# One unit order, one peeled group and one DMA queue changed in an attention and FFN kernel

## The reference

```python
x = x + xattn(layernorm(x), ctx, ctx, pos, mask, Wq, Wk, Wv, Wo)   # x, ctx: 8 x 256 x 1024
x = x + ffn(layernorm(x), qweight, qzeros, scales, bias)           # 1024 -> 1024
# xattn
q = (x @ Wq) -> 32 heads of 128;  k, v = (ctx @ Wk), (ctx @ Wv) -> 8 heads of 128
q, k = q * cos[pos] + rotate_half(q) * sin[pos], the same for k
scores = where(mask == 0, -1e9, q @ k.T / sqrt(128))   # each k, v head serves 4 query heads
return (softmax(scores) @ v) @ Wo
# ffn
return x @ (scales * (4-bit weights - zeros)) + bias
```

## Time and profile before

| what | value |
|---|---|
| median of 3 executions | 2343.98 us (2342.11 to 2347.69) |
| the profiled execution's own time | 2343.98 us |
| PE busy | 2248.4 us, 96% |
| DVE, ACT, POOL busy | 1351.8 us (58%), 1042.3 us (45%), 1379.2 us (59%) |
| DMA moved | 493.52 MB, mean 211 GB/s |

### The profile page before, as it was taken

The page is one execution under the profiler, slowest core; times in us unless marked ns, Lnnn a source line. Parts: engine busy times, 40 slices in busy tenths (PEclk is TensorE's granted clock), DMA queues, the critical chain, the costliest instruction groups (busy, mean ns, idle before and its releaser), DMA issues.

```text
span 2342.2 us, 33158 instructions
## 1 busy us (share of the span) xinstructions
PE 2248.4 (96%) x10560; PEld 1870.0 (80%) x10560; DVE 1351.8 (58%) x2534; ACT 1042.3 (45%) x2264; POOL 1379.2 (59%) x981
## 2 busy tenths in 40 slices
PE   8998999988999999799999999889999999999999
PEld 6887877767888887688888888668887877878887
DVE  4762574767777776577777777537723234443532
ACT  3222123666766675566677667523322222322000
POOL 1320454567888887688888888655654354354220
PEclk9999999999999999999999999999999999999999
DMA  7676675788788778877878887687554454452111
GB/s 270 234 192 208 229 265 184 235 271 275 241 246 252 242 244 278 281 243 242 255 236 250 250 246 246 189 257 267 189 196 158 148 188 153 152 179 99 46 45 45
DMA packets 310494, 493.52 MB, mean 211 GB/s; under 512 B 28176, under 2 KB 200464, under 8 KB 310416
## 3 DMA queue, kind: packets, MB, share of 16 engines
q1 hardware_dynamic: 289680, 440.12, 58.8%
q10 hardware_dynamic: 19968, 50.34, 6.2%
q0 software_dynamic: 768, 2.10, 0.3%
HBM read 312.09 MB, written 180.37 MB: 210 GB/s over the span
## 4 chain that ended last, share of the span: by engine, by line
PE 65%; DMA 9%; POOL 8%; DVE 8%; issue 3%; ACT 3%; SPq 3%; ACTq 0%; POOLq 0%; DVEq 0%
PE ps L227 14%; PE ps L228 14%; PE ps L229 14%; PE ps L763 8%; PE ps L765 8%; PE ps L764 8%; DMA sq_scratch<-scores 5%; POOL q_t L1540 2%; DMA scores<-in_ctx 2%; POOL rope_tmp L1482 2%; SPq L426 1%; DVE rows L1386 1%; POOL s_buf L1482 1%; POOL q_t L1529 1%; DMA left_scratch<-s_buf 1%
## 5 line engine op out<-in xcount | busy, mean ns | idle before, releaser
L227 PE MATMUL ps<-act_t,wq_t 128*128 128x512 f32 x1280 | 502.4, 393 | 8.5 <-DVE wq_t L1302 4.1
L228 PE MATMUL ps<-act_t,wq_t 128*128 128x512 f32 x1280 | 501.2, 392 | 0.0
L229 PE MATMUL ps<-act_t,wq_t 128*128 128x512 f32 x1280 | 499.2, 390 | 0.0
L763 PE MATMUL ps<-b_parts,a_parts 128*128 128x512 f32 x896 | 353.3, 394 | 17.1 <-POOL b_parts L1558 11.0
L1540 POOL TENSOR_TENSOR q_t<-pt_raw,q_t 128x1024 fp32r<-128x1024 f32 x124 | 298.1, 2404 | 112.1 <-ACT q_t L962 111.1
L1558 POOL TENSOR_TENSOR b_parts<-wraw,b_parts 128x512 fp32r<-128x512 f32 x112 | 195.0, 1741 | 276.2 <-ACT b_parts L984 276.2
L1280 DVE TENSOR_TENSOR a_parts<-xring,a_parts 128x1024 fp32r<-128x1024 f32 x112 | 147.4, 1316 | 355.2 <-ACT a_parts L979 355.2
L764 PE MATMUL ps<-b_parts,a_parts 128*128 128x512 f32 x896 | 350.1, 391 | 0.0
L765 PE MATMUL ps<-b_parts,a_parts 128*128 128x512 f32 x896 | 350.0, 391 | 0.0
L979 ACT ACTIVATE a_parts<-xring 128x1024 fp32r<-128x1024 f32 x112 | 118.7, 1060 | 421.7 <-PE ps L765 413.2
L227 PEld LDWEIGHTS ps<-act_t,wq_t 128*128 128x128 f32 x1280 | 242.2, 189 | 57.7 <-issue 4.7
(11 more groups left out here) (120 smaller groups left out, 4344.4 us busy)
## 6 DMA issues: line engine op xcount, KB each, us to landing
sq_scratch<-scores SPq DMA_DIRECT2D x124, 512.0 KB, 4.9
pt_raw<-sq_scratch SPq DMA_DIRECT2D x496, 128.0 KB, 3.1
xring<-left_scratch SPq DMA_DIRECT2D x112, 512.0 KB, 4.0
left_scratch<-s_buf SPq DMA_DIRECT2D x64, 640.0 KB, 5.1
wraw<-in_L_xattn_Wq SPq DMA_DIRECT2D x64, 512.0 KB, 4.8
wraw<-in_L_xattn_Wo SPq DMA_DIRECT2D x64, 512.0 KB, 4.8
v_scratch<-kv_t ACTq DMA_DIRECT2D x32, 512.0 KB, 2.9
k_scratch<-kv_t ACTq DMA_DIRECT2D x32, 512.0 KB, 4.8
```

The source lines that it names most:

```text
L227: eng.matmul(dst, lh, rh, start=(k == first), stop=False)
L228: eng.matmul(dst, lh, rl, start=False, stop=False)
L229: mm = eng.matmul(dst, ll, rh, start=False, stop=(k == last))
L763: pe.matmul(dst, lh, rh, start=(begins and not onto), stop=False, skip_group_check=True)
```

## The change

It has four parts.

1. The pieces: all eight now pass in group 0, one in each unit. SP loads piece u8 at the end of unit u8, ACT stores the parts of piece u8-1 in unit u8 and splits piece u8 at its end. Group 1 is no longer peeled and joins the loop.
2. On ACT, `turned_hi` of the unit before now stands ahead of `query_hi` and `exponents`, in every unit of every group, instead of behind `exponents`.
3. On DVE, `next_head_lo` now stands behind `out_copy` and `inverse_sum`, instead of ahead of them.
4. The 16 loads of the new activations in group 7 are issued by SP, at the start of `u8` 2 and 4, instead of by ACT in the middle of these units.

```diff
@@ -444,12 +444,21 @@
                     sp.wait_ge(parts_stored, i * 32)
                 sp.dma_start(x_pair[0], xc_dram[i]).then_inc(xc_in, 16)
 
-            def attention(G, half, first=False, last=False, switch=False, piece=None):
+            def attention(G, half, first=False, last=False, switch=False):
                 g, nh = (0, 1) if switch else (G - half * 8 + 1, half)
                 for u8 in range(UPG):
                     par, b = u8 // 4, u8 % 4
                     p = (G - half * 8) * 2 + par
                     tail = last and par == 1
+                    if switch and u8 in (2, 4):
+
+                        c = u8 // 2 - 1
+                        sp.wait_ge(q_done, 62 + 2 * c)
+                        sp.wait_ge(parts_stored, 8 * 32)
+                        for k in range(4):
+                            for l in range(2):
+                                sp.dma_start(act_v[:, l, 2 * k:2 * k + 2, c * CT:(c + 1) * CT].bitcast(F32),
+                                             xp_dram[4 * c + k, l]).then_inc(xp_in[4 * c + k], 16)
 
                     if last and u8 == 1:
                         load_step(0)
@@ -486,8 +495,8 @@
                             c = (u8 - 3) // 2
                             sp.wait_ge(q_rot, 62 + 2 * c)
                             sp.dma_start(rope[:, c, :, :], rope_dram[1, c]).then_inc(rope_in[c], 16)
-                    if piece is not None and u8 % 2 == 1 and piece + u8 // 2 < 7:
-                        load_centred(piece + u8 // 2 + 1)
+                    if first and u8 > 0:
+                        load_centred(u8)
                 if last:
                     load_step(2)
                     load_step(3)
@@ -527,9 +536,8 @@
 
             sp.wait_ge(x_lo, TT)
             load_centred(0)
-            attention(0, 0, first=True, piece=0)
-            attention(1, 0, piece=4)
-            with sp.Fori(2, 7) as G:
+            attention(0, 0, first=True)
+            with sp.Fori(1, 7) as G:
                 attention(G, 0)
             attention(7, 0, switch=True)
             with sp.Fori(8, 15) as G:
@@ -983,7 +991,7 @@
                     act.wait_ge(right_in[s % 2], rights_in(s))
                 act.activation(b_parts[:, s % 2, 0, :], wraw[s % 2][:, 0:NW], ACT.Copy).then_inc(right_hi, 1)
 
-            def attention(G, first=False, last=False, switch=False, piece=None):
+            def attention(G, first=False, switch=False, last=False):
                 for u8 in range(UPG):
                     b = u8 % 4
                     tail = last and u8 >= 4
@@ -992,22 +1000,18 @@
                         head_hi(1, G * 32 + (u8 // 4 * 16 + 10 * 16), (q_done, G * UPG + (u8 + 4)))
                     if b == 3 and not last:
                         head_hi(0, G * 32 + (u8 // 4 * 16 + 11 * 16), (q_done, G * UPG + (u8 + 4)))
-                    if piece is not None and u8 % 2 == 1:
-                        store_parts(piece + u8 // 2)
+                    if last and u8 <= 4 or not last:
+                        if u8 > 0:
+                            turned_hi(G, u8 - 1, first=first and u8 < 3)
+                        elif not first:
+                            turned_hi(G - 1, UPG - 1)
+                    if first and u8 > 0:
+                        store_parts(u8 - 1)
                     if not (last and u8 >= 5):
                         i = (u8 + 3) % 4
 
                         scored = G * 16 + (2 * (u8 + 1 - i) + (0 if i < 2 else 4))
                         query_hi(TILES[i], G * UPG + (u8 + 3), None if first and u8 == 0 else scored)
-                    if switch and u8 in (2, 4):
-
-                        c = u8 // 2 - 1
-                        act.wait_ge(q_done, 62 + 2 * c)
-                        act.wait_ge(parts_stored, 8 * 32)
-                        for k in range(4):
-                            for l in range(2):
-                                act.dma_start(act_v[:, l, 2 * k:2 * k + 2, c * CT:(c + 1) * CT].bitcast(F32),
-                                              xp_dram[4 * c + k, l]).then_inc(xp_in[4 * c + k], 16)
                     if u8 < UPG - 1:
                         nxt, nG = u8 + 1, G
                     else:
@@ -1019,19 +1023,14 @@
                         elif not (first and u8 == 0):
                             act.wait_ge(squared, G * UPG + u8)
                         exponents(nG, nxt)
-                    if last and u8 <= 4 or not last:
-                        if u8 > 0:
-                            turned_hi(G, u8 - 1, first=first and u8 < 3)
-                        elif not first:
-                            turned_hi(G - 1, UPG - 1)
                     if tail:
                         tail_high(u8)
                     if last and u8 in (5, 6):
                         step_hi(u8 - 5)
                     if not (last and u8 == UPG - 1):
                         scaled(nG, nxt)
-                    if piece is not None and u8 % 2 == 0:
-                        split_piece(piece + u8 // 2)
+                    if first:
+                        split_piece(u8)
 
 
             act.wait_ge(ident_in, 16)
@@ -1043,9 +1042,9 @@
             exponents(0, 0)
             scaled(0, 0)
             act.wait_ge(rope_stored, 32)
-            attention(0, first=True, piece=0)
-            attention(1, piece=4)
-            with act.Fori(2, 7) as G:
+            attention(0, first=True)
+            store_parts(UPG - 1)
+            with act.Fori(1, 7) as G:
                 attention(G)
             attention(7, switch=True)
             with act.Fori(8, 15) as G:
@@ -1310,7 +1309,7 @@
                     op = dve.tensor_tensor(lo, ps[:, bank, :].rearrange("p (a n) -> p a n", a=4), hi.bitcast(F32), ALU.subtract)
                 op.then_inc(tail_lo, 1)
 
-            def attention(G, half, first=False, switch=False, last=False, piece=None):
+            def attention(G, half, first=False, switch=False, last=False):
                 for u8 in range(UPG):
                     b = u8 % 4
                     tail = last and u8 >= 4
@@ -1326,10 +1325,6 @@
                         nxt, nG, nh = 0, G + 1, 1 if switch else half
                     if not (last and u8 == UPG - 1):
                         masked(nG, nxt, nh, fresh=first and u8 == 0 or last and nxt >= 6)
-                    if b == 0 and not tail:
-                        next_head_lo(1, G * 4 + (2 * (u8 // 4) + 20))
-                    if b == 3 and not last:
-                        next_head_lo(0, G * 4 + (2 * (u8 // 4) + 21))
                     if tail:
                         if u8 < 6:
                             out_copy(G, u8 - 2)
@@ -1346,8 +1341,12 @@
                         set_mask(u8 - 3, 1)
                     if tail:
                         tail_low(u8)
-                    if piece is not None and u8 % 2 == 0:
-                        rest_of_piece(piece + u8 // 2)
+                    if b == 0 and not tail:
+                        next_head_lo(1, G * 4 + (2 * (u8 // 4) + 20))
+                    if b == 3 and not last:
+                        next_head_lo(0, G * 4 + (2 * (u8 // 4) + 21))
+                    if first:
+                        rest_of_piece(u8)
                     if last and u8 in (6, 7):
                         step_lo(u8 - 6)
 
@@ -1361,9 +1360,8 @@
                 query_rot(m % 2, FIRST_TILES[m][1], m, first=(m == 0))
             masked(0, 0, 0, fresh=True)
             inverse_sum(0, 0)
-            attention(0, 0, first=True, piece=0)
-            attention(1, 0, piece=4)
-            with dve.Fori(2, 7) as G:
+            attention(0, 0, first=True)
+            with dve.Fori(1, 7) as G:
                 attention(G, 0)
             attention(7, 0, switch=True)
             with dve.Fori(8, 15) as G:
```

## The result

The changed kernel takes 2444.2 us (median of 4 runs, 2441.5 to 2444.6); the kernel before took 2343.1 us beside it (median of 4, 2337.7 to 2347.7). The ratio is 1.043, 95% interval 1.041 to 1.045: slower, by about 101 us. The forecast was 2395 us with a range up to 2436, so the direction was right and the size was half of what came.

A forecast was written before the change was run, and what follows sets the result against it. The prediction took PE's own pace, 8.26 us a unit, as the bound over most of the kernel. It summed 2344 + 29 (pieces) + 26 (loops) - 4 (switch) = 2395 us, with an 8-in-10 range of 2358 to 2436.

The forecast's parts named there:

- a chain of 16.0 us a link: Group 0: each piece's split, rest, store and next load follow in series, 16.0 us a link, seven links.
- The term was +29: Pieces in group 0: PE starts unit 24 at 659.1 instead of 630.21, +29 us, with +16 and +47 as ends.
- 13 x 2.0 = +26 us: Loops: `turned_hi` ahead of `query_hi` makes the query and one unit 2.0 us late in each of 13 groups.
- SP's lead: Loops: SP's chain falls behind PE over six units and catches up at `u8` 3, having no head, key or value to load.
- The upper end: Loops, parts 2 and 3 together: a two-unit loop with slow landings in every unit, 71.4 us a group, +69 us.
- rival 2: Loops: the two-unit loop binds in every group, +69 instead of +26, total 2438 us; chance 0.12.
- a loop of two units through DRAM: Loops: `turned_hi`, exponentials, scaling, transposes through DRAM, next `turned_hi`: 17.0 us for two units, 18.7 with the head's split, against 16.5.
- -4 forecast: Switch, loads on SP: -1.0 us for each of two batches, about -2 from SP's earlier second lot, -4 us in all.
- 931.7: Switch: time near which the squares' store lands behind SP's eight loads, against 929.15 before, 2.6 us later.
- 941: Switch: time at which SP comes to the second batch of loads, where ACT came at 943.05; about -2 us.
- Rival 3: Switch gets worse, both issue times on SP's chain and both stores late: +18 instead of -4, total 2417 us; chance 0.07.
- The likeliest case: The forecast itself, 2395 us, with +26 for the loops; own range 2375 to 2420, chance 0.52.

The follow-up runs named there:

- Part 1 alone: All eight pieces in group 0, one in each unit, group 1 joining the loop, on the kernel before: 2375.8 us, ratio 1.014.
- part 2 alone: On ACT, `turned_hi` moved ahead of `query_hi` and the exponentials in every unit, on the kernel before: 2407.8 us, ratio 1.026.
- parts 2 and 3: `turned_hi` ahead of `query_hi` and DVE's head split behind the inverse, on the kernel before, pieces and switch unchanged: 2418.1 us, ratio 1.031.
- part 3 alone: DVE's head split (`next_head_lo`) moved behind `out_copy` and `inverse_sum`, on the kernel before: 2342.3 us, ratio 0.998.
- part 4 taken back: The changed kernel with the 16 loads of the switch issued by ACT again instead of SP: 2444.7 us, ratio 1.041.

## Why the prediction fell short

**The pieces: right, but the close hit is in part luck.** Forecast a chain of 16.0 us a link, measured 15.2; PE at unit 24 forecast 659.1, measured 660.9. In between two errors cancel: unit 9, forecast at 535.2, came at 526.6, 8.6 us early, and the 15 units from there to unit 24, forecast at 123.9 us, took 134.3. The term was +29. Part 1 alone gives +28. In the changed kernel groups 0 to 2 take 261.0 us for 227.1, +33.9; less twice 4.6 for the loop's loss in groups 1 and 2 (their units have no pieces, so it should stand there too; that is an inference) it is +24.7.

**The loops: this is the step that failed.** "I count 13 groups (1 to 6 and 8 to 14): 13 x 2.0 = +26 us." The mechanism named, ACT's wait for `pt_raw` holding the query and PE waiting for L1529, is what the run of part 2 alone shows. Its count was wrong, and a second way to PE was left at nothing. Part 2 alone measured +60, parts 2 and 3 +70, a group of the loop 3.7 and, in the changed kernel, 4.6 us instead of 2.0. Two things were missed:
- I took the delay of one unit, `u8` 3, from one row, and supposed that SP's lead heals it once a group. In the run of part 2 alone the lateness is in four units a group, 0.6 to 1.1 us each. A wait that costs nothing in the old order says how late the data comes, not how often; for that all the `turned_hi` of a group were to be read.
- For the sum I followed only the first instruction behind the wait, the query. The exponents stand behind it too, and DVE waits for them at the inverse. Behind the inverse stands the next rotation: `turned_hi` behind the query alone costs +42, and moving the inverse away takes back 40 of it. In the changed kernel the head's split stands there as well, and in its two late units (`u8` 1 and 5) PE waits for it 1.5 us on average.

**The upper end and rival 2 came near by luck.** The upper end had +69 for the two edits, and +70 was measured; rival 2 said 2438, and 2444 came. Its reason was a loop of two units through DRAM. For the 42 us that reason is refuted: the loop would have to bind as well when the inverse is moved, and there the groups run at 66.1 us. With the query behind `turned_hi` too the loop is longer by 0.63 us, and with the head's split longer again; no run moved the inverse in these orders. There the waits for the query and for the split show how PE becomes late, but whether such a loop has a share in how late the bytes land stays open.

**Part 3: I kept nothing for it, and it cost 10 us.** The reason I gave for the upper end ("Now it waits for them, and behind it stand the rotation and transposes of the next unit") is what the rows show. It costs only together with part 2: alone, ratio 0.998, since the exponents are then early; with part 2 DVE reaches the split after 2.35 us of waiting (in the unit shown above), and the split takes 2.09 us on average instead of 1.39, for a reason told at the end. No run tells how the 10 us divide between the later start and the longer split.

**The switch: -4 forecast, about nothing measured.** With and without part 4 the changed kernel has the same time. The working made a gain of 1.0 us a batch, from a store that ends later and turned loads that come sooner; the rows show 22.2 us for 23.0, a gain of 0.8 for the first batch. The store ended 17.8 us from the first load, where I had 931.7 - 915.19 = 16.5, and the turned loads took 4.4 us, not 5.5. (The 931.7 doesn't follow from its own terms: 915.19 + 13.1 + 1.6 is 929.9.) No row that I gave stands behind the 941 for SP's second lot, but that came out too: it began 25.7 us after the first, forecast 25.8, before 27.9. What I hadn't connected is that part 2 puts the query behind this same wait of ACT. Group 7 grew by 4.0 us (by 1.8 with ACT's loads), and by 3.2 already in the run of part 2 alone (91.5 for 88.3). The forecast has the squares' store land behind the bytes of the eight loads on its own queue. No run shows that it must: from the store's issue to that of the turned loads are 11.6 us against 11.5 before, but the one store was issued 6.2 us behind the loads and the other 2.5, so this is no test of it. Rival 3 had +18 us for the switch, from both issue times and both stores late; group 7 grew by 4.0.

**Range and chances.** I put the two missing effects into the upper end (+69) and then gave this end 0.12, because one row looked milder. The likeliest case had nothing for part 3, and the range ended at 2436, short of the upper end itself.

## What to carry to other kernels

When an instruction that waits for a transfer is moved forward on an engine that takes its program in order, list everything that stands behind it, then what each other engine waits for from that list, and what stands behind *those* waits, until the bounding engine is reached; here there were three such paths, all from the same transfer: ACT's and POOL's query to PE; ACT's exponents, DVE's inverse, DVE's rotation and the query to PE; and, with part 3, ACT's exponents, DVE's inverse and DVE's split to PE. Which one PE waits for changes with the order; the transfer in front of them is the same. Price each by its own rows in all units of a period, not in one. Where such a wait can't be avoided, put behind it nothing that the bounding engine needs soon: with `turned_hi` behind the query, moving a 0.18 us reciprocal behind the rotation was worth 40 us, and moving the rest of a piece behind the work that PE waits for was worth 11.

## What the hardware showed

The same split on DVE (128x1024, `wraw` and `wq_t` into fp32r) takes 1394 ns on average before and 1351 in the run of part 2 alone, but 2144 in that of parts 2 and 3 and 2087 in the changed kernel. Its length depends on POOL. Three of the 61 splits of the changed kernel have neither of POOL's two additions of this place (L1527, L1538) beside them, and take 1.20 to 1.21 us. Thirty take 2.5 us or more, and in all thirty POOL's L1538 began first, by 0.3 to 0.9 us. Two such pairs, of the changed kernel: in the first POOL is first, in the second DVE.

```profile
1399.37 2.38 POOL L1538 TENSOR_TENSOR q_t<-pt_raw,q_t 128x1024 fp32r<-128x1024 f32 x1
...
1354.64 1.62 DVE L1301 TENSOR_TENSOR wq_t<-wraw,wq_t 128x1024 fp32r<-128x1024 f32 x1
1355.11 3.43 POOL L1538 TENSOR_TENSOR q_t<-pt_raw,q_t 128x1024 fp32r<-128x1024 f32 x1
```

POOL's instruction ends at 1401.75, and the DVE split of 1400.15 shown above ends at 1402.83, 1.08 us later; in the thirty this distance is 1.07 to 1.10 us. A split with neither addition beside it takes 1.20, so nearly all of DVE's work lies after POOL's end. When DVE is first, its split takes 1.2 to 1.6 us and POOL's addition, 2.4 us otherwise, takes 3.4 (28 pairs, 3.36 to 3.44). So in the changed kernel's pairs it is the one that begins second that takes longer; why is not shown. In the kernel before none of the 61 splits lies beside this addition, and the longest takes 1.94 us. Part 3 puts the split where it meets the addition: in the run of part 3 alone 58 of the 61 do. But there DVE is first in 57 of them, and the mean stays at 1420 ns. Only with part 2 on top, when the inverse comes late, is POOL first in half of the cases (30 of 58; 32 of 58 with parts 2 and 3 alone).

The 16 loads of the switch were issued by ACT in lots of eight (group 7 took 88.3 us before, 85.2 with part 3, 90.1 in the changed kernel with part 4 taken back), by ACT in lots of four (88.8), and by SP (92.3). No order in these lengths goes with who asks for the loads. The share of the DMA engines is 0.87 in the second half of the changed kernel's switch and was 0.91 before; that the bytes set the length is not shown.
